# Sharing the score stage's products, scans and block maxima between engines in a graph-network kernel

## The reference, cut to what matters

```
Q = (h @ Wq).reshape(n, 8, 32);  K = (h @ Wk).reshape(n, 8, 32)
score = einsum('ehd,ehd->eh', K[src], Q[dst]) / sqrt(32) + edge_bias
m = segment_max(score, dst, num_segments=n)
ex = exp(score - m[dst])
```

## Time and profile before

| What | Value |
|---|---|
| Median of 3 timed runs | 7182.26 us (7180.51 to 7193.24) |
| The profiled execution's own time | 7132.51 us |
| Its span, first to last instruction | 7130.8 us |
| Score stage in that span | about 2187 to 3069 us |
| Mean granted TensorE clock, whole span | 0.781 of 2.4 GHz |

### The profile page before, as it was taken

One profiled execution on the slowest core, in us unless ns is written; L12 is line 12 of the kernel. 1 busy time (PEld: TensorE's weight loads), 2 busy tenths in 40 slices (PEclk: granted clock), 3 DMA queues, 4 the chain that ended last, 5 costly groups with the idle time before them and its releaser, 6 DMA issues. The chain is left out here.

```text
span 7130.8 us, 75257 instructions
## 1 busy us (share of the span) xinstructions
PE 4317.0 (61%) x20054; PEld 2955.9 (41%) x20055; DVE 3165.0 (44%) x6539; ACT 1916.6 (27%) x4343; POOL 4465.6 (63%) x4304
## 2 busy tenths in 40 slices
PE   1000588888766666668896455455477767775555
PEld 1000365656534444445674333233344434443333
DVE  5040345544446888878644222222244433333443
ACT  2630355555424555446461000000000000000000
POOL 2677566666546888746313666666566646665666
PEclk6555788888778899989997676767688878887766
DMA  3112122222105666657103445454455544443333
GB/s 85 46 41 54 55 65 67 66 66 67 42 25 178 210 210 213 189 168 215 43 0 122 145 147 140 147 147 146 129 170 176 176 114 133 131 134 97 97 97 87
DMA packets 466880, 826.73 MB, mean 116 GB/s; under 512 B 146229, under 2 KB 316182, under 8 KB 460057
## 3 DMA queue, kind: packets, MB, share of 16 engines
q0 software_dynamic: 209808, 566.12, 27.9%
q1 hardware_dynamic: 256777, 256.98, 11.3%
HBM read 664.90 MB, written 157.90 MB: 115 GB/s over the span
## 5 line engine op out<-in xcount | busy, mean ns | idle before, releaser
L1349 POOL DMA_INDIRECT p_rows<-table,idx_s x1320 | 1292.0, 979 | 773.7 <-issue 372.2
L1394 PE MATMUL p_psA<-p_rows,p_hot 128*128 128x256 bf16 (+1 forms) x4840 | 895.0, 349 | 602.1 <-DMA p_rows<-table,idx_s 401.7
L1394 PEld LDWEIGHTS p_psA<-p_rows,p_hot 128*128 128x128 bf16 (+1 forms) x4840 | 622.1, 134 | 856.2 <-issue 714.3
L585 POOL DMA_INDIRECT p_space<-h_table,p_space x440 | 451.6, 1026 | 289.5 <-issue 126.9
L571 POOL DMA_INDIRECT rec_s<-p_rec_out,p_row_s x416 | 429.8, 1033 | 283.0 <-ACT p_rec_out L696 138.3
L1349 POOL DMA_INDIRECT p_rows<-rel_table,edge_d x440 | 433.8, 986 | 254.0 <-issue 126.2
L655 PE MATMUL p_psW<-p_wf,p_upto 128*128 128x256 f32 x1760 | 480.1, 434 | 183.9 <-DVE p_upto L815 163.3
L376 POOL DMA_INDIRECT rec_d<-edge_d,norm x416 | 426.4, 1025 | 238.2 <-issue 125.3
L1557 POOL DMA_INDIRECT p_rows<-rel_table,edge_d x440 | 437.8, 995 | 219.3 <-issue 129.9
L1423 ACT ACTIVATE sums<-p_psA,inv_degree 128x256 f32<-128x256 f32 x75 | 35.6, 474 | 1850.7 <-DMA p_locs<-loc_rows 963.0
L1777 POOL DMA_INDIRECT p_kg<-kv_table,edge_d x440 | 425.1, 966 | 165.2 <-issue 111.6
(11 more groups left out here) (354 smaller groups left out, 8749.8 us busy)
## 6 DMA issues: line engine op xcount, KB each, us to landing
v_sorted<-p_kg SPq DMA_DIRECT2D x110, 512.0 KB
p_val<-v_sorted SPq DMA_DIRECT2D x110, 512.0 KB
rel_table<-p_o SPq DMA_DIRECT2D x50, 1024.0 KB
p_rows<-table,idx_s POOLq DMA_INDIRECT x1320
p_space<-rec_s SPq DMA_DIRECT2D x110, 136.0 KB
p_locs<-loc_rows SPq DMA_DIRECT2D x110, 128.0 KB, 4.3
p_rows<-rel_table,edge_d POOLq DMA_INDIRECT x880
p_rec_out<-edge_attr SPq DMA_DIRECT2D x103, 128.0 KB
```

The costliest lines, as they stand in the source:

```text
L585: pool.indirect_dma_start(msg[q][:, u, :], None, table, bass.IndirectOffsetOnAxis(ap=rec_i[q][:, u, S_IDX:S_IDX + 1], axis=0))\
L1349: pool.indirect_dma_start(rows[q][:, u, :], None, table, bass.IndirectOffsetOnAxis(ap=idx(n * U + u), axis=0))\
L1394: step = pe.matmul(psA[:, bass.ds(at[u], D)], hot[q][:, u, :], rows[q][:, u, c * D:(c + 1) * D], start=False, stop=(c == terms - 1), skip_ ...
```

## The change

Five edits, all in `score_pass`:

1. `qs` has three buffers (QR = 3). The third lies in a free part of the node table `acc`.
2. VectorE makes the product of every fifth group (n = 4, 9, ..., 109), 22 of 110, at the head of its iteration, ahead of the same group's reduction. GpSimd skips it. `wait_product` picks the semaphore that belongs to a group.
3. `starts` is made before the first group, in the memory of `block_i`.
4. VectorE scans the first CUT = 324 tiles during the stage: one head each behind the finds of groups 81, 84, ..., 102. After the last find it fills one column of `starts` and scans the last 117 columns of each head, beginning with the one that carries the running maximum.
5. The 25 copies to `tops` are shared: ScalarE takes ranks 0 to 9 (two batches), VectorE 10 to 24 (three).

```diff
-    KR, QR, SR, HR, MR = 4, 2, 3, 6, 3
-    half, PAIR = U // 2, 2 * U
+    KR, QR, SR, HR, MR = 4, 3, 3, 6, 3
+    half, PAIR, EVERY = U // 2, 2 * U, 5
...
-        qs = [s.sb(f"qs{q}", [P, U, D]) for q in range(QR)]
+        qs = [s.sb(f"qs{q}", [P, U, D]) for q in range(QR - 1)]
...
+        begun = H * NT + (HR + 1) * row
+        qs.append(flat(acc)[:, begun:begun + U * D].rearrange("p (u f) -> p u f", u=U))
...
-        starts = qs[0][:, :, :].rearrange("p u f -> p (u f)")[:, 0:NT]
+        starts = block_i[:, :].bitcast(F32)
+        CUT = NT // (4 * U) * 3 * U
...
+        def take_tops(engine, kind, ranks, copy):
+
+            for k in ranks:
+                last = load_some(core.nc, kind, plan.last, k, CB, 0, NT - 1)
+                b = load_some(core.nc, kind, plan.order, k, CB, 0, NB - 1)
+                for j in range(CB):
+                    copy(tops[:, bass.ds(b[j] * H, H)], best[:, :, bass.ds(last[j], 1)].rearrange("p h o -> p (h o)"))\
+                        .then_inc(picked, 1)
...
+        own = [n for n in range(groups) if n % EVERY == EVERY - 1]
+
+        def wait_product(engine, n):
+
+            mine = len([m for m in own if m <= n])
+            if n in own:
+                engine.wait_ge(multiplied_here, mine)
+            else:
+                engine.wait_ge(multiplied, n + 1 - mine)
...
+                act.wait_ge(scanned, 2 * H)
+                take_tops(act, ACTE, range(0, NB // (2 * CB) * CB, CB), lambda to, of: act.activation(to, of, ACT.Copy))
...
-                        pool.wait_ge(multiplied, n - KR + 1)
+                        wait_product(pool, n - KR)
...
                 def multiply(n):
+                    if n in own:
+                        return
...
+                link(dve.memset(starts[:, :], -BIG))
+                link(dve.tensor_tensor(starts[:, 1:NT], g.blk_d[:, 1:NT], g.blk_d[:, 0:NT - 1], ALU.not_equal))
+                link(dve.tensor_scalar(starts[:, 1:NT], starts[:, 1:NT], -BIG, None, ALU.mult))
+
+                def multiply(n):
+                    if n not in own:
+                        return
+                    q = n % KR
+                    dve.wait_ge(gathered[q], (n // KR + 1) * (16 * U))
+                    dve.wait_ge(q_in, 2 * (n + 1))
+                    a = qs[n % QR][:, :, :]
+                    dve.tensor_tensor(a, kg[q][:, :, 0:D], a, ALU.mult).then_inc(multiplied_here, 1)
 
                 def reduce(n):
-                    dve.wait_ge(multiplied, n + 1)
+                    wait_product(dve, n)
...
+                def scan(n):
+                    h = (n - CUT // U) // 3
+                    if n < CUT // U or n % 3 or h >= H:
+                        return
+                    dve.wait_ge(found, CUT)
+                    dve.tensor_tensor_scan(best[:, h, 0:CUT], starts[:, 0:CUT], best[:, h, 0:CUT], 0.0, ALU.add, ALU.max)\
+                        .then_inc(scanned, 1)
+
+                unrolled(groups, [(3, multiply), (3, reduce), (3, finish), (3, divide(0)), (0, find(0)), (3, divide(1)), (3, divide(2)),
+                                  (0, find(1)), (3, divide(3)), (3, divide(4)), (0, find(2)), (0, find(3)), (0, scan)])
+
                 dve.wait_ge(found, U * groups)
+                link(dve.memset(starts[:, CUT - 1:CUT], -BIG))
                 for h in range(H):
-                    link(dve.tensor_tensor_scan(best[:, h, :], starts[:, :], best[:, h, :], 0.0, ALU.add, ALU.max))
...
+                    step = dve.tensor_tensor_scan(best[:, h, CUT - 1:NT], starts[:, CUT - 1:NT], best[:, h, CUT - 1:NT], 0.0,
+                                                  ALU.add, ALU.max)
+                    link(step, scanned, H + h + 1)
+                take_tops(dve, DVE, range(NB // (2 * CB) * CB, NB, CB), lambda to, of: dve.tensor_copy(to, of))
```

More of the change, by code:

```diff
@@ L1704, in score_pass @@
         dividing = [s.sem(f"dividing{k}") for k in range(4)]
-        spread, found = s.sem("spread"), s.sem("found")
+        spread, found, scanned = s.sem("spread"), s.sem("found"), s.sem("scanned")
+        def take_tops(engine, kind, ranks, copy):
[5 more added lines that the diff above has]
+                        .then_inc(picked, 1)
         cleared, opened, chosen, typed, picked, dve_step = (
             s.sem(n) for n in ("cleared", "opened", "chosen", "typed", "picked", "dve_step"))
+        multiplied_here = s.sem("multiplied_here")
+        own = [n for n in range(groups) if n % EVERY == EVERY - 1]
[5 more added lines that the diff above has]
+                engine.wait_ge(multiplied, n + 1 - mine)
         by_tile = hotT[HR - 1][0:groups]
```

## The result

Before 7180.51 us (median, 7169.04 to 7193.24), after 7217.13 us (7210.66 to 7228.2): ratio 1.0052, 95% interval 1.0038 to 1.0065. The change costs 37 us, where I forecast 11 gained; the time lies outside my range. Later runs met a second kind of chip, on which the same changed kernel is no slower than before (0.9991, 0.9982 to 1.0000). What parts the two kinds is the subject of this part.

A forecast was written before the change was run, and what follows sets the result against it. GpSimd, at 7.28 us a group, was taken to bound the score stage, by only 0.13 us over a query loop. The terms 0 + 2.1 - 1.4 - 5.4 - 6.3 = -11.0 us gave 7171.3 us; range 7128 to 7198.

The forecast's parts named there:

- Every fifth product on VectorE: Score stage: 4.4 us lost on the query loop, 4.3 gained as slow-level lateness misses VectorE's own products; together 0.
- the loop: Score stage, once per group: reduction, find, show, expand, query copy, product, next reduction; mean 7.15 us against GpSimd's 7.28.
- Third buffer: Score stage, query copies wait for the reduction three groups back instead of two: worth 0, between 0 and 21.4 us.
- Scans during the stage: Eight scans of 0.83 us behind finds of the score stage, partly fitting VectorE's slack: 2.1 us lost, between 0 and 6.6.
- Block starts, end scans, shared maxima: End of the stage: gains of 1.4 us from early starts, 5.4 from shorter scans, 6.3 from copies shared with ScalarE.
- The sum: Whole kernel: 0 + 2.1 - 1.4 - 5.4 - 6.3 = -11.0 us, giving 7171.3 us.
- the real relief of GpSimd: Rival, chance 0.17: in the score stage copies could come early, 55 us gained, with the tail 66: 7116 us.
- The rival of the held product: Rival, chance 0.10: each VectorE product in the score stage waits out one gather, 0.95 us, 21 us in all; 7192.
- TensorE's slow level: Rival, chance 0.10: longer TensorE waits make slow matmuls commoner in the score stage, 1.06 us per further group; up to 7218.
- ordinary products 7.3 us apart: Sign that the forecast is right: in the score stage, ordinary GpSimd products stay 7.3 us apart.
- GpSimd's waits of some 65 us: Sign of being right: GpSimd waits about 2 us for the copy after each skipped product, some 65 in total, before 22.9.
- The stretch within 5 us: Sign of being right: first product to last find takes as long as before, within 5 us.

The follow-up runs named there:

- 14: Kernel before, VectorE making every fifth product and GpSimd a 0.62 us idle operation where it skips its own; quicker kind of chip: stage 837.7 us, ratio 1.0000.
- 6: Kernel before, GpSimd skipping every fifth product and VectorE making a one-input reduction of equal length instead; quicker kind of chip: stage 838.2 us, ratio 1.0005.
- experiment 16: Kernel before with only the early block starts and the copies shared with ScalarE; quicker kind of chip: stage 835.7 us, ratio 0.9988.
- experiment 3: Changed kernel without products on VectorE, GpSimd making all 110; slower kind of chip: stage 844.1 us, ratio 0.9985.
- 10: Kernel before with only every fifth product moved to VectorE, on chip 1, of the slower kind: stage 886.9 us, ratio 1.0071.
- 2: Kernel before with only every fifth product moved to VectorE, on chip 7, of the slower kind: stage 902.3 us, ratio 1.0094.
- experiment 4: Kernel before with early block starts, eight scans in the stage and short ones at the end; slower kind of chip: stage 842.6 us, ratio 0.9999.
- 9: Kernel before, unchanged, traced again on chip 1, of the slower kind: stage 835.7 us.
- 1: Kernel before, unchanged, traced again on chip 7, of the slower kind: stage 831.9 us.
- experiment 5: Kernel before, every fifth product skipped by GpSimd and made by nobody; quicker kind of chip: stage 801.5 us, ratio 0.9953.
- experiment 17: Changed kernel as it is, on the quicker kind of chip: stage 844.0 us, ratio 0.9991.
- experiment 11: Kernel before, VectorE making every fifth product and GpSimd waiting for it where it skips its own; slower kind of chip: stage 842.7 us, ratio 1.0013.

## Why the prediction was wrong

By its own steps:

- **Every fifth product on VectorE, 0: wrong on the L chips, and this is most of the miss** (42.6 us against a miss of 48; the size of the scans makes most of the rest). The price was right (1.22 forecast, 1215 ns), and so nearly was the plain loss on the loop: on P 2 to 3 us of stage (14 and 6 against 16). I had signalling from ScalarE's copy to a waiting product at 0.06 us; the rows have 0.14 (2310.56 to 2310.70), which makes the loop 7.23 us, as good as GpSimd's 7.28, and this term some 2 us. The step that failed is the sentence that GpSimd "has two batches of gathers done early and waits about 2 us for that copy". I took the two batches as free, and the loop as long as ever, and never asked what eight gathers in a row would do to others. On the L chips the signals of TensorE come late in such a run, so the copy does too: GpSimd's wait behind a skipped product has a median of 4.7 us there, and 2.65 on P. My rows showed steady groups with four gathers; the twelve at the stage's opening, with the late copy at 2207.00, stood in the same profile. With the third buffer this costs 886.7 - 844.1 = 42.6 us of stage (the result's trace against experiment 3), without it 51 to 70 us (10, 2).
- **Third buffer, 0.** Alone it was not run. Beside the late signals it may help, which is not shown: experiments 2 and 10 have 902.3 and 886.9 us without it, the changed kernel 886.7 with it and with some 10 us of scans on top, but each on another chip.
- **Scans during the stage, +2.1: mis-sized.** 7 to 11 us (experiment 4 against 9 and 1), above my upper bound of 6.6 us. 0.83 us each became a mean of 1.55 (result) to 1.85 (experiment 3), up to 2.07, since most waited GpSimd's product out.
- **Block starts, end scans, shared maxima, -1.4, -5.4, -6.3: right but for 1.1 us.** In all 12.0 us measured at the end (24.2 to 12.2) against 13.1; experiment 4 shows the first two, 6.8, and experiment 16 the first and last: 24.2 to 17.5. The 1.1 is in the shared maxima: VectorE's first batch now starts 2.63 us behind the scans, where it was 1.45.
- **The sum** on an L chip: +42.6 + 12.2 (scans and third buffer, 844.1 - 831.9) - 12.0 = +42.8 us, measured +37 (27 to 47). On a P chip: 844.0 - 835.7 - 12.0 = -4 us, measured -6 (-12 to 0).

Of the rivals, the real relief of GpSimd (7116) is what experiment 5 shows only where nobody makes the product. The rival of the held product is refuted by its own sign: no product on VectorE took over 1.22 us (1.200 to 1.218), where over 1.5 would have shown it. What was held was the gather issued beside it (mean 1.47 us in the result, ordinarily 0.95), and its price is not to be seen: on P it costs nothing that can be told, and on L the kernel without it is no faster. TensorE's slow level grew by little (granted clock 0.91 to 0.89, and 0.90 in experiment 17), so what I had as the other side was the wrong mechanism. Of my signs, ordinary products 7.3 us apart held on both kinds (median 7.29); GpSimd's waits of some 65 us held on P (71.5) and were 110 on L. The stretch within 5 us failed on L (+51.7) and on P (+8, about what the scans cost).

One row looks like a hint and is none. Waits of ScalarE's query copy, first in before's steady part, then in experiment 16 from 1880 to 2760 us, which is a P chip:

```profile
ACT p_qs L1757 <- issue: 255.8, 78, 10.1
ACT p_qs L1757 <- PE p_psQ L1831: 104.8, 61, 4.4
```

```profile
ACT p_qs L1779 <- PE p_psQ L1857: 365.0, 146, 9.8
...
ACT p_qs L1779 <- issue: 4.2, 2, 2.4
```

On P the profile puts this wait down to TensorE, on L mostly to "issue", which reads like late signals. But take the copy at 2855.91, idle 3.19 us "issue". Its matmuls are

```profile
2855.05 0.82 PE L1831 MATMUL p_psQ<-q_parts,sums 128*128 x6
```

They end at 2855.87, 0.04 us before the copy: it was in time. So it is with all of the copies in before's stage that are booked so; none starts over 0.15 us behind its matmuls. What differs is the record: the trace of before keeps 39254 semaphore changes and that of experiment 16 keeps 90760, with about as many instructions, and where a change is missing the profile can't name who ended the wait. A late signal shows in the time from a matmul's end to the start of what waited for it, not in the name that the wait is booked under. In before's steady part such waits cost next to nothing: its stage is as long on L as on P.

## What to carry to other kernels

Taking an operation out of an engine's list also changes the order of what is left: look for what now stands back to back that never did, DMA issues above all, and try a break there (the wait of experiment 11 took the loss from 51 us of stage to 7). A VectorE instruction with two SBUF inputs that is laid into another engine's loop is to be priced by what GpSimd does at that moment, not by its own size. To see whether a wait's end was late, compare it with the end of what it waited for. And a change of less than 1% should be tried on more than one chip: here it is 0.5% slower on one kind and no slower on the other.

## What the hardware showed that was not expected

- Chips of two kinds: the same kernel before took 7135 and 7193 us on two of them and 6481 to 6487 on three others. In the traces of the slower kind, waits on TensorE's results end up to several us behind its last matmul, with "remote" or a foreign DMA as releaser; with eight gathers in a row it is 19 to 21 finds, 32 to 47 us in the stage. On the quicker kind none of the finds has such a wait. What makes the kinds differ no run shows.
- On the slower kind signals were 3 to 6 us late in runs of eight indirect gathers 0.30 us apart, and 3.8 to 4.1 us late in a run of twelve with VectorE idle; with four, a pause of 3.83 us and four more no find was over 1.4 us late.
- A 128x324 scan took 0.82 us alone and up to 2.07 beside GpSimd's 128x1024 product. A gather took 0.95 us, a mean of 1.40 to 1.47 beside VectorE's 128x1024 product with two inputs, and 0.95 beside a reduction of the same length with one.
